# Mixers of a two-layer decoder: ScalarE copies one PSUM bank of four per head, GpSimd multiplies it with the queries in place of VectorE

## The reference

```
kv = jnp.einsum('bhil,bhjl->bijhl', k_, v_)
kv_f = jnp.fft.rfft(kv, n=fft_size)
kernel_f = jnp.fft.rfft(ssm_kernel, n=fft_size)
y = jnp.fft.irfft(kv_f * kernel_f, n=fft_size)[..., :L]
out = y + kv * D[None, None, None, :, None]
out = jnp.einsum('bijhl,bhil->bjhl', out, q_)
```

## Time and profile before

| | us |
|---|---|
| median of 3 runs | 941.39 |
| lowest and highest | 937.65 to 943.47 |
| the profiled execution | 937.29 |
| its span in the trace | 935.4 |
| mixer m0, first outer product to VectorE's last sum | 221.39 to 314.79 |
| mixer m1, first outer product to VectorE's last sum | 621.84 to 714.75 |

### The profile page before, as it was taken

The page is one execution under the profiler, slowest core; times in us unless marked ns, Lnnn a source line. Parts: engine busy times, 40 slices in busy tenths (PEclk is TensorE's granted clock), DMA queues, the critical chain, the costliest instruction groups (busy, mean ns, idle before and its releaser), DMA issues. The chain is left out here.

```text
span 935.4 us, 12527 instructions
## 1 busy us (share of the span) xinstructions
PE 795.8 (85%) x4171; PEld 526.3 (56%) x4218; DVE 699.0 (75%) x1401; ACT 405.6 (43%) x638; POOL 499.0 (53%) x582
## 2 busy tenths in 40 slices
PE   6999999995999598898789999869994578777784
PEld 4666666652444276676567777634441256555563
DVE  3667677761999776574689999828996699999974
ACT  1444444454100155543388778610000256666664
POOL 2443355424777244341246787867771366666661
PEclk9999999997999799999699999889997599999997
DMA  5440000003000400000121112000001000000000
GB/s 177 181 160 12 13 12 13 6 1 135 0 1 0 171 2 0 2 1 1 48 90 46 46 65 72 2 0 1 0 0 32 11 18 12 23 24 23 17 18 24
DMA packets 16080, 34.18 MB, mean 37 GB/s; under 512 B 2961, under 2 KB 11921, under 8 KB 14737
## 3 DMA queue, kind: packets, MB, share of 16 engines
q1 hardware_dynamic: 15152, 25.96, 8.2%
q10 hardware_dynamic: 864, 7.41, 2.0%
HBM read 31.20 MB, written 2.16 MB: 36 GB/s over the span
## 5 line engine op out<-in xcount | busy, mean ns | idle before, releaser
L371 POOL TENSOR_TENSOR at_kbd<-at_qk,at_hmask 128x1024 f32<-128x1024 f32 x32 | 60.0, 1896 | 103.7 <-DVE at_qk L339 103.7
L935 PE MATMUL ss_b<-XT,win_late 128*128 128x256 f32 x320 | 89.0, 410 | 4.5 <-DVE ss_xc L1151 4.2
L313 DVE TENSOR_REDUCE at_mx<-at_b 128x4 f32<-128x512 f32 x64 | 44.2, 690 | 56.0 <-PE at_b L179 56.0
L466 PE MATMUL m_y<-m_kv,toep 128*128 128x512 f32 x128 | 67.5, 609 | 10.8 <-POOL m_kv L455 10.8
L486 DVE TENSOR_REDUCE MIX<-m_pr 128x128 f32<-128x1024 f32 x64 | 74.7, 1208 | 0.0
L455 POOL TENSOR_TENSOR m_kv<-XT,CTXT 128x1024 f32<-128x1024 f32 x32 | 61.6, 1946 | 23.2 <-PE m_y L468 20.2
L455 POOL TENSOR_TENSOR m_kv<-CTXT 128x1024 f32<-128x1024 f32 x32 | 59.8, 1892 | 25.1 <-PE m_y L468 22.3
L294 ACT COPY at_pt<-at_b 128x512 f32<-128x512 f32 x64 | 37.3, 585 | 77.9 <-PE at_b L186 77.9
L1151 DVE SCALAR_TENSOR_TENSOR ss_xc<-ss_b,cw_late,ss_xc 128x254 f32<-128x254 f32 x144 | 66.6, 477 | 4.7 <-ACT ss_xc L1041 1.1
L935 PEld LDWEIGHTS ss_b<-XT,win_late 128*128 128x128 f32 x320 | 59.1, 201 | 19.0 <-DVE ss_xc L1151 11.3
L179 PE MATMUL at_b<-at_kbd,at_qk 128*128 128x512 f32 x128 | 66.1, 598 | 3.4 <-POOL at_kbd L371 2.3
(11 more groups left out here) (231 smaller groups left out, 1955.5 us busy)
## 6 DMA issues: line engine op xcount, KB each, us to landing
MIX<-cum_rows SPq DMA_DIRECT2D x16, 512.0 KB, 3.7
at_xT<-xT_dram SPq DMA_DIRECT2D x16, 128.0 KB, 2.6
X<-x_dram SPq DMA_DIRECT2D x1, 2048.0 KB, 10.5
MIX<-wgu_dram ACTq DMA_DIRECT2D x1, 2048.0 KB, 7.9
toep<-toep_dram ACTq DMA_DIRECT2D x1, 2048.0 KB, 15.4
CTXT<-ctxT_dram ACTq DMA_DIRECT2D x1, 2048.0 KB, 18.5
toep<-toep_dram SPq DMA_DIRECT2D x1, 2048.0 KB, 9.7
f_ct<-ctx_dram SPq DMA_DIRECT2D x16, 128.0 KB, 2.1
```

Of the source, the lines that this page charges most:

```text
L371: m = nc.gpsimd.tensor_tensor(KBD[k][:, g, :, :], QK[k][:, 2 + g, :].unsqueeze(1).broadcast_to([P, G0, S]), hmask[:, :].unsqueeze(2).broad ...
L466: nc.tensor.matmul(bY[k][0][h][:, :], toep[:, a, 0:P], kv[0], start=True, stop=True)
L935: m = nc.tensor.matmul(bX[(NU * g + n) % 3][:, 0:GS_], win[:, h, off:off + P], XT[:, h, bass.ts(g, GS_)], start=(h == 0), stop=(h == C - 1))
```

## The change

In each head, the bank of the second half c = 1, h = 1 is no longer read by VectorE. ScalarE copies it to a new SBUF tile `EV` of two buffers (`lift`, semaphore `lifted`), and GpSimd multiplies that with the queries into the same part of `PR` (`times_q`, semaphore `pool_multed`). GpSimd does so for head a-1 after it has made the outer products of head a. VectorE's sum for c = 1 of head a is moved behind the products and the first sum of head a+1, and waits for GpSimd's product; at the end both sums of the last head are made. In m0 the copies are interleaved with ScalarE's sums of weights, four behind each. TensorE waits for three products of VectorE of head a-2 instead of four, and for the copy.

```diff
--- before.py
+++ after.py
@@ -411,16 +411,17 @@
 
 
     nc = ch.nc
+    HB = B // 2
     KV = [ch.sb(f"{name}_kv{k}", [P, C, B * J, J]) for k in range(2)]
     PR = [ch.sb(f"{name}_pr{k}", [P, C, B * J, J]) for k in range(2)]
     bY = [[[ch.bank(f"{name}_y{k}{c}{h}") for h in range(2)] for c in range(C)] for k in range(2)]
-    kv_made, conved, multed, reduced = (ch.sem(f"{name}_{n}") for n in ("kv_made", "conved", "multed", "reduced"))
+    EV = [ch.sb(f"{name}_ev{k}", [P, HB * J * J]) for k in range(2)]
+    kv_made, conved, multed, reduced, lifted, pool_multed = (ch.sem(f"{name}_{n}") for n in ("kv_made", "conved", "multed", "reduced", "lifted", "pool_multed"))
     signed, staged_in, w_summed = (ch.sem(f"{name}_{n}") for n in ("signed", "staged_in", "w_summed"))
     junk = ch.sb(f"{name}_junk", [P, C * FF], BF16) if skip else None
     MIX, CTXT, XT = T["MIX"], T["CTXT"], T["XT"]
     kt = CTXT if skip else XT
     qt = XT if skip else CTXT
-    HB = B // 2
 
     def head(t):
         return t[:, :, :].rearrange("p c (b h j) -> p c h b j", b=B, h=HM)
@@ -435,6 +436,11 @@
 
         @block.scalar
         def _(act):
+            def lift(a):
+                act.wait_ge(conved, a + 1)
+                upto(act, pool_multed, a - 1)
+                nc.scalar.copy(EV[a % 2][:, :], bY[a % 2][1][1][:, :]).then_inc(lifted, 1)
+
             if skip:
                 nc.scalar.activation(T["wgu0"][:, :, :], T["MIX"][:, :, :], ACT.Sign).then_inc(signed, 1)
                 nc.scalar.activation(T["wd0"][:, :, :], T["wd0"][:, :, :], ACT.Sign)
@@ -443,9 +449,22 @@
                     upto(act, w_summed, k)
                     nc.scalar.activation(junk[:, :], T[n][:, :, :].rearrange("p r w -> p (r w)"), ACT.Abs,
                                          accum_out=T["wpart"][:, k:k + 1]).then_inc(w_summed, 1)
+                    for a in range(4 * k, 4 * k + 4):
+                        lift(a)
+            for a in range(12 if skip else 0, HM):
+                lift(a)
 
         @block.gpsimd
         def _(pool):
+            def times_q(a):
+                if a < 0:
+                    return
+                pool.wait_ge(lifted, a + 1)
+                upto(pool, reduced, 2 * a - 1 if a > 1 else 0)
+                q = head(qt)[:, 1, a, HB:B, :].unsqueeze(2).broadcast_to([P, HB, J, J])
+                nc.gpsimd.tensor_tensor(PR[a % 2][:, 1, bass.ts(1, HB * J), :].rearrange("p (b j) i -> p b j i", b=HB),
+                                        EV[a % 2][:, :].rearrange("p (b j i) -> p b j i", b=HB, j=J), q, ALU.mult).then_inc(pool_multed, 1)
+
             for a in range(HM):
                 k = a % 2
                 upto(pool, conved, a - 1)
@@ -454,13 +473,16 @@
                     vj = head(CTXT)[:, c, a, :, :].unsqueeze(3).broadcast_to([P, B, J, J])
                     m = nc.gpsimd.tensor_tensor(KV[k][:, c, :, :].rearrange("p (b j) i -> p b j i", b=B), ki, vj, ALU.mult)
                 m.then_inc(kv_made, 1)
+                times_q(a - 1)
+            times_q(HM - 1)
 
         @block.tensor
         def _(pe):
             for a in range(HM):
                 k = a % 2
                 pe.wait_ge(kv_made, a + 1)
-                upto(pe, multed, 4 * a - 4)
+                upto(pe, multed, 3 * a - 3)
+                upto(pe, lifted, a - 1)
                 for h in range(2):
                     kv = [KV[k][:, c, bass.ts(h, HB * J), :] for c in range(C)]
                     nc.tensor.matmul(bY[k][0][h][:, :], toep[:, a, 0:P], kv[0], start=True, stop=True)
@@ -470,21 +492,29 @@
 
         @block.vector
         def _(dve):
+            def add_up(a, c):
+                if a < 0:
+                    return
+                dve.wait_ge(multed, 3 * a + 2 + c)
+                if c:
+                    dve.wait_ge(pool_multed, a + 1)
+                nc.vector.tensor_reduce(head(MIX)[:, c, a, :, :], PR[a % 2][:, c, :, :].rearrange("p (b j) i -> p b j i", b=B),
+                                        op=ALU.add, axis=AX.X).then_inc(reduced, 1)
+
             for a in range(HM):
                 k = a % 2
                 dve.wait_ge(conved, a + 1)
-                for c in range(C):
-                    for h in range(2):
-                        q = head(qt)[:, c, a, bass.ts(h, HB), :].unsqueeze(2).broadcast_to([P, HB, J, J])
-                        nc.vector.tensor_tensor(PR[k][:, c, bass.ts(h, HB * J), :].rearrange("p (b j) i -> p b j i", b=HB),
-                                                bY[k][c][h][:, :].rearrange("p (b j i) -> p b j i", b=HB, j=J),
-                                                q, ALU.mult).then_inc(multed, 1)
+                upto(dve, reduced, 2 * a - 1 if a > 1 else 0)
+                for c, h in ((0, 0), (0, 1), (1, 0)):
+                    q = head(qt)[:, c, a, bass.ts(h, HB), :].unsqueeze(2).broadcast_to([P, HB, J, J])
+                    nc.vector.tensor_tensor(PR[k][:, c, bass.ts(h, HB * J), :].rearrange("p (b j) i -> p b j i", b=HB),
+                                            bY[k][c][h][:, :].rearrange("p (b j i) -> p b j i", b=HB, j=J),
+                                            q, ALU.mult).then_inc(multed, 1)
                 if skip and a == 0:
                     dve.wait_ge(signed, 1)
-                for c in range(C):
-                    dve.wait_ge(multed, 4 * a + 2 * c + 2)
-                    nc.vector.tensor_reduce(head(MIX)[:, c, a, :, :], PR[k][:, c, :, :].rearrange("p (b j) i -> p b j i", b=B),
-                                            op=ALU.add, axis=AX.X).then_inc(reduced, 1)
+                add_up(a, 0)
+                add_up(a - 1, 1)
+            add_up(HM - 1, 1)
 
 
 class Chain:
```

## The result

The changed kernel takes 958.5 us (median of 4 runs, 955.29 to 958.75) against 942.11 for the kernel before (4 runs): a ratio of 1.0171, interval 1.0140 to 1.0203. A second round of both on another occasion gave 955.37 (4 runs) against 943.15 (17 runs), 1.0145, interval 1.0104 to 1.0186. Both intervals are 95% intervals and lie above 1: it is slower, by 12 to 16 us. The profiled execution took 958.75 us, with a span of 956.8.

A forecast was written before the change was run, and what follows sets the result against it. TensorE bounds the mixers without a gap. Late outer products, ScalarE's pass and the tail, 6.0 + 0.4 + 0.5 and 6.8 + 0.5, make +14.3 us: 951.6 from the profiled execution, 955.7 against the median; range 949 to 961.

The forecast's parts named there:

- the +14.3 of the forecast: Both mixers: 6.0 + 0.4 + 0.5 us in the first, 6.8 + 0.5 in the second, with roundings.
- rival 1: Cheap multiplication on GpSimd, 1.04 or 0.94 us with shortest hand-overs; chain 5.42 to 5.51, +9 to +10 us; chance 0.14.
- rival 3: Slow multiplication, 1.6 us, or contention, hand-overs of 0.18 everywhere; up to +20 us, 961; chance 0.14.
- The removed product: One of VectorE's four products per head, about 0.62 us: worth nothing inside the mixer, something in the tail.
- The chain: Release of head a through copy, multiplication and outer products to TensorE's head a+2: 5.81 us against 4.95 allowed; second mixer 5.92.
- The cost of a stall: TensorE starts a late head 0.86 us late in the first mixer, 0.97 in the second; seven times each, 6.0 and 6.8.
- The alternation: Only every second head, 2, 4, ... 14, is late: seven per mixer; VectorE idle about 1.4 us per head.
- ScalarE's pass in front of the first copy: First mixer: head 0's copy stands behind ScalarE's first sum of weights, so head 2 comes another 0.4 us later.
- The tail: VectorE's work after a mixer's last release: three products and three sums, 5.25 us instead of 4.73, +0.5 per mixer.
- rival 2: Not slower: GpSimd's multiplication streams like its one-input row, 0.47 us; +3 us, 944.5; chance 0.08 with other ways.
- The clock stayed at 1.00: Against the rival that TensorE's clock falls in the stalls, 2.27 us each, 32 us in all: 988; chance 0.03.
- The price by elements: GpSimd at about 2.6 cycles per element: multiplication 1.11 us without fixed part, sum about +12 us; trace contradicts a flat price.

The follow-up runs named there:

- the first pair: First profiles of the kernel before and of the changed kernel, no further edit; medians 942.11 and 958.5 us, ratio 1.0171.
- the second pair: Both kernels profiled and timed again without edit: changed kernel 955.37 us against 943.15 for the kernel before, ratio 1.0145.
- the relief alone: Kernel before with VectorE's fourth product left out and made by nobody, its place set to zero once; 936.61 us, one run.
- the half-multiplication kernel: Changed kernel with GpSimd's multiplication over half of its bank, 128x256; 949.27 us against 942.72 for the kernel before, ratio 1.0085.

## Why the prediction was right

Forecast 955.7 us, measured 958.5 and 955.4. The mechanism was right: TensorE waited for GpSimd's outer products, at every second head, and moving the multiplication one place later in GpSimd's list took the loss away. That the mixers of the first pair grew by just the +14.3 of the forecast is partly luck. Their bodies grew by 13.6, and the starts, for which nothing was forecast, made up the other 0.65; in the second pair the bodies grew by 13.8 and the mixers by 15.2. Three slips in the working change nothing: the page's shares are an average over six stages, not five; the upper chain of rival 1 adds up to 5.52 us, not 5.51; and both additions of rival 3 together give +21, not +20. By the forecast's steps:

- **The removed product: nothing inside, a little in the tail.** Right; the relief alone gave 0.59 and 0.60 us.
- **The chain.** Forecast 5.81 us, found 5.68. ScalarE wakes with VectorE, at 0.00 and not 0.05. From the release to the multiplication is 0.66 and not 0.74 (the second wait, met long before, costs nothing that shows). The first outer product starts 1.23 us behind the multiplication's start, 0.04 before its row ends. The multiplication was forecast at 1.27 from the streamed kind of the earlier trace rows, and took 1.27.
- **The cost of a stall.** Here two small errors met and nearly cancelled, which is luck. The shorter chain makes head 2 late by 5.68 - 4.95 = 0.73 us, not 0.86. But the head that stalled is also longer: 242.18 to 247.44 is 5.26 us, not 5.15, and its first product pair reads 1.12 in place of 1.02. With these 0.11 us a stall costs 0.84. Times seven it is 5.9, and 0.95 x 7 = 6.6 in the second mixer, against my 6.0 and 6.8. The bodies less the tail give 5.9 and 6.7.
- **The alternation.** Right: seven waits of the products in each mixer, between unhindered heads, and VectorE idle for 1.85 and 1.01 us in turn, 1.4 on the mean.
- **ScalarE's pass in front of the first copy.** Forecast +0.4. In the first profile it didn't come: the pass ended at 236.41, just before the release at 236.50. In the second it cost 0.22 (the copy at 233.15, the release at 232.93, and a body of 88.61 against 88.40), in the half-multiplication kernel 0.65. When the weights land and how long the low-clock start takes differ between executions, so this term of the sum was not a constant; forecast at 0.4, it was 0, 0.2 and 0.65.
- **The tail.** Forecast 5.25 us, found 5.26:

```profile
319.64 1.89 DVE L510 TENSOR_TENSOR m_pr<-m_y,XT 128x512 f32<-128x512 f32 x3 [1.02 <-PE m_y L490]
...
321.44 3.46 DVE L501 TENSOR_REDUCE MIX<-m_pr 128x128 f32<-128x1024 f32 x3
```

- **The rivals.** The cheap multiplication fell (1.27 us); it needs a standing operand, and then it is 1.08. With it fell rival 2, which needed less than 0.92. The slow one and contention fell: VectorE's products kept 680 to 692 ns and GpSimd's 1266 to 1278. The clock stayed at 1.00, so a wait of 0.6 us every 11 us doesn't bring it down here.
- **The price by elements.** The rows of 256 and 512 streamed elements, 0.73 and 1.27 us, make 2.1 ns an element and 0.19 us fixed; 2048 elements would then take an estimated 4.5 us, and the row has 4.53. The Trainium skill (GPSIMD Engine Reference, 3.1 Elementwise) has about 2.6 cycles of a 1.2 GHz clock for each element of a two-input operation, from which 1.11 us was estimated for 512 elements without a fixed part. The rate of these rows, 2.5 such cycles, agrees with it; the fixed part was what that estimate lacked.

## What to carry to other kernels

Before moving work to an idle engine, look at what stands behind it in that engine's own list, and whether somebody on the bound waits for that. Here GpSimd had 1.4 us to spare in each head and the new work needed 1.3, yet its place in the list cost 12.6 us over the two mixers, and one place later nothing; VectorE's longer tail, 1.1 us in all, stayed in both. And relieving VectorE, for which nobody waited inside the mixers, was worth only its tail; where the bound engine has no gap, the ends of the stage are what can be had.

## What was not expected of the hardware

- A wait of TensorE costs more than its length: after each, the head took 5.26 us in place of 5.15, at a granted clock of 1.00. The first weight load of that head starts with its product, at 242.18; in the kernel before it starts 0.43 us ahead of it (242.48 against 242.91), under the products of the head before. I read the 0.11 us as this load no longer being hidden; no run tests that by itself.

```profile
242.18 0.30 PEld L488 LDWEIGHTS m_y<-m_kv,toep 128*128 128x128 f32 x2 [1.40 <-POOL m_kv L474]
```
```profile
242.48 0.19 PEld L466 LDWEIGHTS m_y<-m_kv,toep 128*128 128x128 f32 x1 [0.24 <-issue]
```

- GpSimd's time at a fixed number of elements follows the access pattern: 1.27 us with both operands streamed, 1.08 with one of them standing still innermost, in the same place of the same kernel.
- The low-clock start of a mixer took between 6.87 and 8.48 us to the first release in profiles of nearly the same code, and attention differs by 3 us between two profiles of one kernel. A difference of a few us between single spans says nothing; the bodies, at a clock of 1.00, repeat to within 0.01 us where the start doesn't reach into them.
